# Weight loads of an attention and mixture-of-experts layer cut by output column instead of by input row, with a wait for each piece

## What is computed

```python
x = x + _L0_attn_ref(_layernorm(x), W_qkv, W_proj, b_proj)
x = x + _L0_ffn_ref(_layernorm(x), router_w, up_w, down_w)

# attention, per head (q and k through relu, a row of ones added to v)
vk  = einsum('bhdn,bhne->bhde', v, k)
out = einsum('bhde,bhen->bhdn', vk, q)
out = out[:, :, :-1] / (out[:, :, -1:] + 1e-15)
y   = out @ W_proj.T + b_proj

# experts: softmax of the router, the 4 largest weights, made to sum to 1
h = gelu(einsum('bsd,edh->bseh', x, up_w))      # 8 experts, 1024 -> 4096
o = einsum('bseh,ehd->bsed', h, down_w)         # 4096 -> 1024
output = sum over the 4 chosen experts of weight * o
```

## Time and profile before

| | us |
|---|---|
| time before, median of 2 runs | 4574.85 |
| the 2 runs | 4538.58 and 4611.12 |
| the profiled execution | 4536.99 |
| its span, slowest core (core 5) | 4535.4 |
| spans of the 8 cores | 4526.4 to 4535.4 |

### The profile page before, as it was taken

The page is one execution under the profiler, slowest core; times in us unless marked ns, Lnnn a source line. Parts: engine busy times, 40 slices in busy tenths (PEclk is TensorE's granted clock), DMA queues, the critical chain, the costliest instruction groups (busy, mean ns, idle before and its releaser), DMA issues.

```text
span 4535.4 us, 48572 instructions; the slowest of 8 cores (4526.4 to 4535.4 us)
## 1 busy us (share of the span) xinstructions
PE 4089.7 (90%) x18704; PEld 1815.9 (40%) x18704; DVE 1115.5 (25%) x2372; ACT 834.1 (18%) x1398; POOL 109.5 (2%) x153
## 2 busy tenths in 40 slices
PE   3995554369999999999999999999999999999989
PEld 1442111134444444444444444444444444444434
DVE  1322344512222222222222222222222222222212
ACT  1331211111111111111111111111111111111111
POOL 0000000000000000000000000000000000000000
PEclk7997666689999999999999999999999999999999
DMA  5131110141313232323222222222232323131321
GB/s 89 29 56 24 28 37 28 46 99 37 75 38 74 46 67 47 66 52 61 56 56 56 56 56 56 56 56 56 56 65 48 65 47 72 41 75 38 78 71 38
DMA packets 113632, 249.16 MB, mean 55 GB/s; under 512 B 3584, under 2 KB 20096, under 8 KB 113408
## 3 DMA queue, kind: packets, MB, share of 16 engines
q0 software_dynamic: 67024, 157.31, 20.2%
q1 hardware_dynamic: 46384, 88.74, 5.7%
HBM read 390.76 MB, written 12.58 MB: 89 GB/s over the span
## 4 chain that ended last, share of the span: by engine, by line
PE 89%; DVE 5%; DMA 4%; issue 1%; ACT 1%; DVEq 0%; ACTq 0%; SPq 0%; POOLq 0%
PE ps L938 39%; PE ps L973 39%; PE ps L307 5%; PE ps L679 1%; DMA wqkv<-wqkvT 1%; DMA xf32h<-xT 1%; DMA w<-upw 1%; PE ps L153 1%; PE ps L608 1%; DVE qp L557 0%; PE ps L157 0%; DMA xbfA<-xT 0%; PE ps L917 0%; DVE gcmp L778 0%; PE ps L336 0%
## 5 line engine op out<-in xcount | busy, mean ns | idle before, releaser
L938 PE MATMUL ps<-y_pair,w 128*128 128x512 bf16 x8192 | 1784.4, 380 | 0.0
L973 PE MATMUL ps<-gh,dn_bf 128*128 128x512 bf16 x8192 | 1773.3, 379 | 0.0
L973 PEld LDWEIGHTS ps<-gh,dn_bf 128*128 128x128 bf16 x8192 | 801.6, 98 | 966.5
L938 PEld LDWEIGHTS ps<-y_pair,w 128*128 128x128 bf16 x8192 | 797.6, 98 | 970.3 <-issue 21.8
L949 ACT ACTIVATE gt<-ps 128x512 bf16<-128x512 f32 x1024 | 611.9, 598 | 1159.4 <-PE ps L938 1157.2
L957 DVE TENSOR_TENSOR gh<-gt,ge 128x512 bf16<-128x512 bf16 x1024 | 435.7, 426 | 1442.1 <-ACT gt L949 1442.1
L981 DVE TENSOR_TENSOR acc<-acc,ps 128x512 f32<-128x512 f32 x512 | 352.3, 688 | 1400.4 <-PE ps L973 1397.3
L926 ACT CAST ge<-ps 128x512 bf16<-128x512 f32 x64 | 37.3, 583 | 1764.1 <-PE ps L917 1764.1
L307 PE MATMUL ps<-wqkv,xlnA 128*128 128x512 bf16 x1024 | 228.8, 382 | 41.4 <-DMA wqkv<-wqkvT 41.0
L307 PEld LDWEIGHTS ps<-wqkv,xlnA 128*128 128x128 bf16 x1024 | 98.5, 98 | 163.9 <-issue 53.5
L679 PE MATMUL ps<-xlnB,w 128*128 128x512 bf16 x256 | 65.2, 422 | 62.0 <-DVE xlnB L233 62.0
(11 more groups left out here) (85 smaller groups left out, 676.7 us busy)
## 6 DMA issues: line engine op xcount, KB each, us to landing
y_pair<-yscr SPq DMA_DIRECT2D x32, 2048.0 KB, 11.8
w<-upw POOLq DMA_DIRECT2D x64, 1024.0 KB, 8.4
dn_bf<-downw POOLq DMA_DIRECT2D x64, 1024.0 KB, 8.4
xbfA<-xT POOLq DMA_DIRECT2D x8, 1024.0 KB, 8.8
xf32h<-xT SPq DMA_DIRECT2D x16, 512.0 KB, 3.7
outT<-acc SPq DMA_DIRECT2D x4, 2048.0 KB, 7.3
wqkv<-wqkvT POOLq DMA_DIRECT2D x4, 1536.0 KB, 11.3
x_bfB<-xT POOLq DMA_DIRECT2D x4, 1024.0 KB, 9.2
```

What stands on the lines that cost most here:

```text
L938: li = nc.tensor.matmul(bk[:, 0:512], up_bf[:, cc * 2048 + hc * 128: cc * 2048 + (hc + 1) * 128], y_pair[:, cc * 1024 + (t % 2) * 512: cc ...
L973: li = nc.tensor.matmul(bk[:, 0:512], dn_bf[:, hc * 1024 + oc * 128: hc * 1024 + (oc + 1) * 128], gh2[t % 2][:, hc * 512:(hc + 1) * 512], ...
```

## The change

The same three arrays are loaded in four transfers each, on the same queue and in the same order, but cut by output column: a transfer brings, for all the blocks of input rows, a quarter of the columns that are used. A transfer of `up_bf` is now 128 x 8 x 512 elements instead of 128 x 2 x 2048, one of `dn_bf` 128 x 16 x 256 instead of 128 x 4 x 1024. Both carry as many bytes as before, in runs a quarter as long and four times as many. A transfer of `wqkv` is 128 x 8 x 512 instead of 128 x 2 x 3072: the q columns, which stage A doesn't read, are no longer loaded. PE waits before the first group that reads a piece, in the first tile only, for that piece alone. A tensor `epsb` is added and filled once, with a wait-free marker behind it; nothing reads it.

```diff
+        nc.vector.memset(epsb[:, :], EPS_ATTN)
+        ev_epsb = sv.inc(nc.vector.engine_nop())
...
                 for og in range(4):
                     gi = t * 16 + sub * 4 + og
+                    if t == 0 and sub == 0:
+                        nc.tensor.wait_ge(sg.sem, wqkv_parts[og])
...
+            wqkv_parts = []
             for i in range(4):
                 sg.dma(nc.gpsimd,
-                    AP(wqkv, i * 2 * 3072, [[CCH * 3072, 128], [3072, 2], [1, 3072]]),
-                    AP(wqkvT, i * 2 * 128 * 3072,
-                       [[3072, 128], [128 * 3072, 2], [1, 3072]]))
+                    AP(wqkv, 1024 + i * 512,
+                       [[CCH * 3072, 128], [3072, CCH], [1, 512]]),
+                    AP(wqkvT, 1024 + i * 512,
+                       [[3072, 128], [128 * 3072, CCH], [1, 512]]))
+                wqkv_parts.append(sg.n)
...
             for t in range(NT_A):
-                if t == 0:
-                    nc.tensor.wait_ge(sg.sem, ev_wqkv)
                 nc.tensor.wait_ge(sv.sem, ev_xln_t[t])
...
                 for hc in range(HCH):
+                    if t == 0 and hc % 4 == 0:
+                        nc.tensor.wait_ge(sg.sem, EB_C["up_parts"][hc // 4])
...
                 for oc in range(CCH):
+                    if t == 0 and oc % 2 == 0:
+                        nc.tensor.wait_ge(sg.sem, EB_C["dn_parts"][oc // 2])
...
+                up_parts = []
                 for i in range(4):
                     sg.dma(nc.gpsimd,
-                        AP(up_bf, i * 2 * 2048,
-                           [[CCH * 2048, 128], [2048, 2], [1, 2048]]),
-                        AP(upw, e * C * Hf + hh * 2048 + i * 2 * 128 * Hf,
-                           [[Hf, 128], [128 * Hf, 2], [1, 2048]]))
-                ev_up_ld = sg.n
+                        AP(up_bf, i * 512,
+                           [[CCH * 2048, 128], [2048, CCH], [1, 512]]),
+                        AP(upw, e * C * Hf + hh * 2048 + i * 512,
+                           [[Hf, 128], [128 * Hf, CCH], [1, 512]]))
+                    up_parts.append(sg.n)
                 if s >= 1:
                     nc.gpsimd.wait_ge(st.sem, ev_dn_used[s - 1])
+                dn_parts = []
                 for i in range(4):
                     sg.dma(nc.gpsimd,
-                        AP(dn_bf, i * 4 * 1024,
-                           [[HCH * 1024, 128], [1024, 4], [1, 1024]]),
-                        AP(downw, e * Hf * C + (hh * 2048 + i * 4 * 128) * C,
-                           [[C, 128], [128 * C, 4], [1, 1024]]))
-                ev_dn_ld = sg.n
-
-                nc.tensor.wait_ge(sg.sem, ev_up_ld)
+                        AP(dn_bf, i * 256,
+                           [[HCH * 1024, 128], [1024, HCH], [1, 256]]),
+                        AP(downw, e * Hf * C + hh * 2048 * C + i * 256,
+                           [[C, 128], [128 * C, HCH], [1, 256]]))
+                    dn_parts.append(sg.n)
...
                     EB_C["ypair_free"] = st.n
-                    if tp2 == 0:
-                        nc.tensor.wait_ge(sg.sem, ev_dn_ld)
                     c_down(s, t0)
```

More of the change, by code:

```diff
@@ L93, in build_program @@
         bproj = Ecm(nc.sbuf_tensor("bproj", [128, 8], F32))
+        epsb = Ecm(nc.sbuf_tensor("epsb", [128, 1], F32))
         rw = Ecm(nc.sbuf_tensor("rw", [128, 8 * E], BF16))
@@ L998, in build_program @@
                     nc.gpsimd.wait_ge(st.sem, ev_up_used[s - 1])
+                up_parts = []
                 for i in range(4):
                     sg.dma(nc.gpsimd,
-                        AP(up_bf, i * 2 * 2048,
-                           [[CCH * 2048, 128], [2048, 2], [1, 2048]]),
-                        AP(upw, e * C * Hf + hh * 2048 + i * 2 * 128 * Hf,
-                           [[Hf, 128], [128 * Hf, 2], [1, 2048]]))
-                ev_up_ld = sg.n
+                        AP(up_bf, i * 512,
[3 more added lines that the diff above has]
+                    up_parts.append(sg.n)
                 if s >= 1:
                     nc.gpsimd.wait_ge(st.sem, ev_dn_used[s - 1])
+                dn_parts = []
                 for i in range(4):
                     sg.dma(nc.gpsimd,
-                        AP(dn_bf, i * 4 * 1024,
-                           [[HCH * 1024, 128], [1024, 4], [1, 1024]]),
-                        AP(downw, e * Hf * C + (hh * 2048 + i * 4 * 128) * C,
-                           [[C, 128], [128 * C, 4], [1, 1024]]))
-                ev_dn_ld = sg.n
-                nc.tensor.wait_ge(sg.sem, ev_up_ld)
+                        AP(dn_bf, i * 256,
[3 more added lines that the diff above has]
+                    dn_parts.append(sg.n)
+                EB_C["up_parts"], EB_C["dn_parts"] = up_parts, dn_parts
                 if s == 0:
```

## The result

| | before | changed |
|---|---|---|
| ratio of the times, 95% interval | 1 | 0.9927 (0.9902 to 0.9951) |
| fastest of the runs, first comparison | 4536.8 | 4500.4 |
| profiled execution | 4537.0 | 4504.8 |
| its span, slowest core | 4535.4 | 4503.3 |

The changed kernel is 0.73% faster, 33 us of 4538. The profile is of core 1, the slowest; the lines of this kernel stand 1 to 11 higher than before.

A forecast was written before the change was run, and what follows sets the result against it. The prediction took PE's work to bound the kernel, leaving only its pauses for weights to shorten. From the profiled 4537.0 us, -12 (stage A), -22 (stage C's first step), 0 (later steps) and +1 (waits) gave 4504 us, range 4494 to 4555.

The forecast's parts named there:

- What bounds the kernel: Whole span: PE works 90%; only its pauses can shrink, with weight waits of 43.0 us (stage C) and 41.0 (stage A).
- PE doesn't pause, so 15 of the 16 steps have nothing to give: Later stage C steps: weight loads are issued 55 us before PE wants them, so the change gains 0.
- Stage A, -12: Start of stage A: pieces of `wqkv` at a period of 10.0 us save 12 us, ends -15 and -9.
- about 1 us of slow clock still to come: Stage A, after the first 32 matmuls: about 1 us of slow clock remains that before lay inside their 9.35 us.
- Stage C, -22: First step of stage C: PE starts with the first `up_bf` piece; first `c_up` ends at 950.4 instead of 972.5.
- The period of 11: `dn_bf` loads in stage C: 10.2 us landing from work per run, 10.7 with a gap, taken as 11.
- The cover that the forecast worked out: `dn_bf` in stage C: no waiting below a period of 14.0 us in the first step, 19.0 in later ones.
- Waits on PE, +1: Stages A and C: 99 more waits on PE at 0.013 us each cost 1 us.
- 1 and 2: Stage C `dn_bf` loads: period above 19.0 us pauses all steps (4844 at 24; 3%); 17.6 costs only the first (4519; 10%).
- Rival 3: Starts of stages A and C: pieces slow, period 13.9 us each; 4531 us, chance 10%.
- Rival 4: First `c_up` of stage C: clock stays low while PE stops and goes, -1.5 instead of -22; 4525 us, chance 7%.
- Rival 5: Both starts: the change doesn't do what it says, PE still begins with the last piece; about 4537 us, chance 4%.

The follow-up runs named there:

- experiment 3: Changed kernel, but stage A waits for the last `wqkv` piece ahead of its first product, still without q columns; 4509.2 us in its one run.
- experiment 6: Changed kernel with `dn_bf` cut once more, into 8 pieces of 128 columns, a wait ahead of each `c_down` group; 4510.1 us in its one run.
- experiment 7: Changed kernel, but the first step's `up_bf` is loaded during stage B, after the last projection; fastest run 4497.6 us, ratio 0.9931 to the kernel before.

## Why the prediction was right

The forecast was 4504.0 us against the profiled 4537.0, a ratio of 0.9927; the ratio measured is 0.9927. Part of that agreement is luck. Over the eight cores stage A gave 14.8 us instead of 12 and the first step of stage C 20.1 instead of 22; stage B, which the sum put at nothing, took 2.2, and the waits 0.3 at most instead of 1. The errors cancel to under 1 us.

- *What bounds the kernel.* Right for the weights: the gain lies in the two starts, and all from the first `c_down` on changed by 0.1 us (3535.0 and 3534.9). But "PE doesn't pause, so 15 of the 16 steps have nothing to give" overlooks a pause that has nothing to do with weights. In the last step PE waits for its second `y_pair`, 16.7 to 18.2 us on each core of both kernels. Before, on core 5:

```profile
PE ps L917 <- DMA y_pair<-yscr: 16.8, 1, 16.8
```

```profile
4369.72 28.00 SPq L58 DMA_DIRECT2D outT<-acc  x2
4405.17 0.37 SPq L58 DMA_DIRECT2D y_pair<-yscr  x1
```

 The load stands on SP's queue behind two stores of the output, each of which waits for the last add of its tile's `c_down`, and it goes out when the second, issued at 4397.7, has landed. In the other steps this load goes out when the `c_down` ahead begins. No run tried another order.
- *Stage A, -12.* It was -15.9 at the first `kv_sub` and -14.8 at the stage's end. The mechanism held, the length of a piece was mis-sized: I took a period of 10.0 us between the 9.2 of later x loads and the 10.8 of the second x load, and it was 9.3, 9.0, 9.2 and 8.9. The first two x loads are slow for a reason that no run shows, and the row nearest in time was the wrong neighbour here. The median of all x loads (8.8) would have been nearer, but isn't a law either: in the changed kernel it is 10.5 on this core beside 8.6 for the `wqkv` pieces of the same shape. The "about 1 us of slow clock still to come" holds as an average: on cores 0, 3, 4 and 7 the products behind the first `kv_sub` still run slowly (on core 0 the granted clock is 0.50 until 69 us) and cost 2.0 us, on the other four nothing. That makes most of the step from 15.9 to 14.8. That the loaded bytes and not the waits would carry most of it (experiment 3) the forecast's sum contained, but its text didn't say so.
- *Stage C, -22.* It was -20.1 on average and -16.0 between the two profiled cores. The term that was off is the landing of the pieces: the last one came 44.8 us after the first issue on average, 43.2 were forecast. On core 1 it is above all the first piece, beside `y_pair`: 13.7 + 1.0 us forecast, 17.8 measured, as the chain shows (over the eight cores 12.9 to 17.8, on average 15.3):

```profile
883.94 17.78 DMA w<-upw
...
902.25 10.28 DMA w<-upw
...
913.06 9.29 DMA w<-upw
```

 Pieces two and three, 10.3 and 9.3 us, are also above the 9.0 of the forecast (on average 9.5 and 9.3). The forecast let the gate start with the first piece. It doesn't wait for `up_bf` any more, and `y_pair` releases it, on this core 3.6 us before the first `c_up` and on the others 11.6 to 16.6 us after line 842; that changes nothing, as `c_up` waits for the piece.
- *`dn_bf`.* The period of 11 from the work per run was 10.0 on average over all steps and cores (9.2 to 11.6), the landing 9.5 instead of 10.2, and nothing waited. The cover that the forecast worked out (14.0 in the first step, 19.0 later) wasn't reached, so where it ends wasn't tested; experiment 6 shows only that twice as many transfers still fit in the later steps.
- *Waits on PE, +1.* Nothing of it can be seen in 3534.9, and 0.3 at most in the average.
- *Rivals.* 1 and 2 are excluded by a landing of 9.5 us. `dn_bf` was loaded beside DVE's products without waiting for them, so the rule of the Trainium skill (SBUF — State Buffer, "SBUF: two separate sides") did no harm here. The forecast had read it too widely: DVE's products and adds are `TENSOR_TENSOR`, which the same page of the Trainium skill ("Who interferes with whom") says has no 2-port mode. Rival 3 (a period of 13.9 for each piece at the start of a stage) didn't come: the periods are 8.5 to 9.8 us in stage A, and in stage C 9.2 to 11.6 behind the first piece. Rival 4 (low clock) holds for a small part, below. Rival 5 is excluded by PE's four bursts.

## What to carry to other kernels

When a load ahead of a stage is exposed, look first at whether all of its bytes are read, and then at whether the consumer can begin with a piece: here the unread third of `wqkv` was worth 10.5 us and its four waits 5.4. A cut by consumption order pays only where the wait is exposed; here it shortened two waits of some 40 us and changed nothing in the 15 steps whose loads had 55 us of cover. Nor did it cost anything there, since runs a quarter as long made a load only 7 to 13% longer. A load that is moved earlier into a quiet stretch needs a look at the short transfers on the critical chain that it will meet, as in experiment 7.

## What was not expected of the hardware

TensorE's granted clock falls more readily than the forecast took it to. In the first `c_up` of the changed kernel, core 1, stretches of the windows view (length, PE, weight loads, DVE, ACT, POOL, then the clock, the DMA share and GB/s) read:

```profile
901.00:905.00 4.00, 3.15 (x8) 1.12 (x9) 0.00 (x0) 0.00 (x0) 0.87 (x1) 0.53 0.07 2
905.00:910.00 5.00, 4.61 (x22) 1.98 (x21) 0.78 (x2) 2.96 (x4) 0.00 (x0) 1.00 1.07 147
...
930.00:932.00 2.00, 0.22 (x2) 0.13 (x3) 0.43 (x1) 0.41 (x1) 0.00 (x0) 1.00 0.40 66
932.00:936.00 4.00, 4.00 (x12) 1.47 (x11) 0.06 (x1) 0.60 (x1) 1.14 (x1) 0.57 0.49 46
936.00:941.00 5.00, 5.00 (x24) 2.07 (x22) 1.22 (x3) 1.51 (x3) 0.00 (x0) 1.00 1.28 172
```

It came to full speed (2.4 GHz) behind the first products. After three pauses of 1.9 to 2.8 us it was near its lower level of 1.2 GHz (0.57) for 4 us in the midst of work, and came back. The last 32 products took 8.75 us instead of 7.07, so on this core the stop-and-go start costs 1.7 us more than its pauses. Six of the other seven cores have one such block behind their first, of 8.5 to 9.5 us. On five of these another wait for a piece follows and hides it: their first `c_up` ends 7.2 us after the last landing, that of cores 1 and 0 after 8.9 and 8.7. In stage A of core 1 the three groups of 8 products behind pauses of 5.5 to 7.2 us take 3.4 to 3.6 us each (granted clock 0.50 to 0.56), the one behind a pause of 2.3 us takes 2.7 (0.67).
